# Attention probabilities turned by VectorE and a way through memory

## The reference

```
x      = rmsnorm(layernorm(x)) * w
h_q    = (x @ w_q.T).reshape(b, 128, 32, 128)      # queries
h_k    = (ctx @ w_k.T).reshape(b, 128, 32, 128)    # keys
h_v    = (ctx @ w_v.T).reshape(b, 128, 32, 128)    # values
score  = einsum('bqhd,bkhd->bhqk', h_q, h_k) + position_bias
prob   = softmax(where(mask, score, -inf), axis=-1)
attn   = einsum('bhqk,bkhd->bqhd', prob, h_v)
out    = attn @ w_out.T
```

## Time and profile before

| | us |
|---|---|
| median of 3 runs (970.29 to 971.5) | 970.51 |
| the profiled execution | 970.3 |
| its span, first to last instruction | 968.5 |
| TensorE busy | 959.6 |
| VectorE / ScalarE / GpSimd busy | 565.8 / 433.1 / 495.8 |
| one loop pass (group 3: 335.49 to 435.17) | 99.68 |

### The profile page before, as it was taken

How to read it: one execution, slowest core, us unless ns; L and a number is a source line. 1 busy time by engine, 2 the same in 40 slices (tenths; PEclk the granted TensorE clock), 3 DMA queues, 4 the chain that set the end, 5 groups by cost and what they waited for, 6 DMA issues and landing times.

```text
span 968.5 us, 15533 instructions
## 1 busy us (share of the span) xinstructions
PE 959.6 (99%) x5042; PEld 814.8 (84%) x5042; DVE 565.8 (58%) x972; ACT 433.1 (45%) x1128; POOL 495.8 (51%) x463
## 2 busy tenths in 40 slices
PE   9999899999999999999999999999999999999998
PEld 8888788888888888888888888888888888888885
DVE  5878844375437543754376436653566866756654
ACT  5774524352534343534444334433443337646630
POOL 3756653355336543745374636463546325697630
PEclk9999999999999999999999999999999999999999
DMA  7133565456555555665556555665557544200002
GB/s 280 45 131 152 205 237 222 178 218 235 205 218 206 217 217 206 238 217 217 195 219 247 217 195 195 249 238 195 195 210 281 188 158 175 88 23 1 1 1 87
DMA packets 50100, 174.28 MB, mean 180 GB/s; under 512 B 6800, under 2 KB 7056, under 8 KB 49040
## 3 DMA queue, kind: packets, MB, share of 16 engines
q1 hardware_dynamic: 49056, 172.50, 48.0%
q10 hardware_dynamic: 1008, 1.32, 0.4%
HBM read 162.26 MB, written 11.53 MB: 179 GB/s over the span
## 4 chain that ended last, share of the span: by engine, by line
PE 94%; DVE 4%; ACT 1%; DMA 1%; issue 1%; SPq 0%; DVEq 0%
PE bank L1870 27%; PE bank L1886 18%; PE bank L1939 17%; PE bank L2046 10%; PE bank L1903 6%; PE bank L1923 6%; PE bank L1846 4%; PE bank L1914 3%; PE bank L2070 2%; DVE work_raw L1426 1%; PE bank L2199 1%; PE bank L2136 1%; PE bank L2156 1%; DMA craw<-in_ctx 1%; DVE acc L1363 0%
## 5 line engine op out<-in xcount | busy, mean ns | idle before, releaser
L561 POOL TENSOR_TENSOR wvo<-stage,wvo 128x512 fp32r<-128x512 f32 x64 | 82.7, 1316 | 195.7 <-ACT wvo L862 195.7
L1939 PE MATMUL bank<-wvo,ao 128*128 128x512 f32 x768 | 180.2, 392 | 1.2 <-DVE acc L1363 1.2
L1886 PE MATMUL bank<-wvo,ct 128*128 128x512 f32 x768 | 177.8, 390 | 0.0
L1939 PEld LDWEIGHTS bank<-wvo,ao 128*128 128x128 f32 x768 | 142.9, 188 | 30.8 <-issue 1.6
L1886 PEld LDWEIGHTS bank<-wvo,ct 128*128 128x128 f32 x768 | 143.5, 188 | 29.4
L1870 PE MATMUL bank<-ring,wkq 128*128 128x512 f32 x648 | 159.0, 393 | 0.0
L1870 PEld LDWEIGHTS bank<-ring,wkq 128*128 128x128 f32 x648 | 120.2, 188 | 24.3
L1363 DVE SCALAR_TENSOR_TENSOR acc<-bank,gated_rows,acc 128x512 f32<-128x512 f32 x128 | 95.5, 748 | 48.4 <-PE bank L1939 47.7
L904 ACT ACTIVATE bank<-prob,nmax 128x128 f32<-128x128 f32 x256 | 91.4, 357 | 36.9 <-DVE nmax L1339 36.9
L1354 DVE TENSOR_TENSOR ao<-bank,ao 128x512 fp32r<-128x512 f32 x64 | 44.0, 691 | 109.3 <-ACT ao L910 109.0
L1385 DVE TENSOR_TENSOR qt<-bank,qt 128x512 f32<-128x512 f32 x98 | 66.4, 690 | 54.8 <-PE bank L1870 52.5
(11 more groups left out here) (185 smaller groups left out, 1574.1 us busy)
## 6 DMA issues: line engine op xcount, KB each, us to landing
ring<-combined SPq DMA_DIRECT2D x216, 512.0 KB, 6.2
stage<-in_w SPq DMA_DIRECT2D x63, 512.0 KB, 3.5
combined<-work SPq DMA_DIRECT2D x16, 512.0 KB, 3.4
xraw<-in_x SPq DMA_DIRECT2D x2, 1024.0 KB, 11.4
bias<-in_bias SPq DMA_DIRECT2D x8, 256.0 KB, 3.5
cs<-in_ctx SPq DMA_DIRECT2D x1, 2048.0 KB, 7.9
out<-acc SPq DMA_DIRECT2D x8, 256.0 KB, 2.0
craw<-in_ctx ACTq DMA_DIRECT2D x4, 256.0 KB, 6.1
```

Source lines behind the costliest of these rows:

```text
L561: pool.tensor_tensor(wvo[:, 1, h, :], stage[:, vo_stage(g, m, c)[0], :], wvo[:, 0, h, :].bitcast(fp32), ALU.subtract).then_inc(s_vo_lo, 1)
L1886: mm = pe.matmul(bank[un_of[m][u] % RING][:, :], ct[:, i, c, b * P:(b + 1) * P], wvo[:, j, c, :], start=(c == 0 and i + j == 0), stop=(c = ...
L1939: mm = pe.matmul(bank[to][:, :], ao[:, h, p, b * P:(b + 1) * P], wvo[:, j, 2 * pair + h, :], start=(h == 0 and p + j == 0), stop=(h == 1 a ...
```

## The change

Nothing is turned on TensorE any more, and `pt_out` is gone. Scores stay in their PSUM bank: bias and mask are added in place, the exponentials too. `softmax_out` writes the probabilities to `turned_blocks` in the order block column j, b, k, and then VectorE transposes them in squares of 32x32. To make a full transpose of these, the squares have to change places between groups of 32 partitions. That is done by a DMA to memory (`passing`, 512 KB a head, two buffers) and four DMAs back into `keyed`, each into 32 partitions. `attend` waits for these and reads `keyed`, with the 128 queries of a block as four runs of 32. `turned_blocks` and `keyed` exist once: a head's multiplication waits until the head before is in memory, and a head's way back waits for the attend of the head before.

```diff
-    prob = place("prob", [P, 2, B, P], fp32)
+    turned_blocks = place("turned_blocks", [P, 4, B, 32], fp32)
+    keyed = place("keyed", [P, 4, B, 32], fp32)
...
+    passing = nc.dram_tensor("passing", (2, 4, 32, 4, B * 32), fp32, kind="Internal").ap()
...
+                def passed(g, h):
+                    sp.wait_ge(s_turned, g * 2 * GH + 2 * h + 2)
+                    sp.dma_start(passing[h % 2, :, :, :, :].rearrange("i k j c -> (i k) j c"),
+                                 turned_blocks[:, :, :, :].rearrange("p j b q -> p j (b q)")).then_inc(s_passed, 16)
+
+                def back(g, m, h):
+                    sp.wait_ge(s_passed, 16 * (g * GH + h) + 16)
+                    if (m, h) != ("first", 0):
+                        sp.wait_ge(s_pv, g * 2 * GH + 2 * h)
+                    for j in range(4):
+                        sp.dma_start(keyed[32 * j:32 * j + 32, :, :, :].rearrange("k i b q -> k i (b q)"),
+                                     passing[h % 2, :, :, j, :].rearrange("i k c -> k i c")).then_inc(s_keyed, 16)
...
-                def pt_out(g, h):
-                    for s in range(2):
-                        act.wait_ge(s_pt, g * 2 * GH + 2 * h + s + 1)
-                        act.activation(prob[:, h % 2, 4 * s:4 * s + 4, :], bank[6 + s][:, :].rearrange("p (b k) -> p b k", b=4),
-                                       ACT.Copy).then_inc(s_pte, 1)
...
-                def softmax_out(g, h, s):
+                def softmax_out(g, m, h, s):
...
                     dve.reciprocal(rinv[:, bs], esum[:, bs]).then_inc(s_rinv, 1)
+                    if s == 0 and (m, h) != ("first", 0):
+                        dve.wait_ge(s_passed, 16 * (g * GH + h))
                     dve.wait_ge(s_rinv, n + 1)
-                    dve.tensor_tensor(prob[:, h % 2, bs, :], bank[4 + s][:, :].rearrange("p (b k) -> p b k", b=4),
-                                      rinv[:, bs].unsqueeze(2).to_broadcast([P, 4, P]), ALU.mult).then_inc(s_p, 1)
+                    dve.tensor_tensor(turned_blocks[:, :, bs, :].rearrange("p j b k -> p b j k"),
+                                      bank[4 + s][:, :].rearrange("p (b j k) -> p b j k", b=4, j=4),
+                                      rinv[:, bs].unsqueeze(2).unsqueeze(3).to_broadcast([P, 4, 4, 32]), ALU.mult).then_inc(s_p, 1)
+                    dve.wait_ge(s_p, n + 1)
+                    dve.transpose(turned_blocks[:, :, bs, :], turned_blocks[:, :, bs, :]).then_inc(s_turned, 1)
...
                 def attend(g, h):
                     if h == 0:
                         pe.wait_ge(s_val_out, 8 * g + 8)
+                    pe.wait_ge(s_keyed, 64 * (g * GH + h) + 64)
                     for s in range(2):
-                        pe.wait_ge(s_pte, g * 2 * GH + 2 * h + s + 1)
+                        pe.wait_ge(s_aolo, g * 2 * GH + 2 * h + s + 1)
                         for b in range(4 * s, 4 * s + 4):
                             mm = pe.matmul(bank[6 + s][:, (b - 4 * s) * P:(b - 4 * s + 1) * P],
-                                           vals[:, b, h * P:(h + 1) * P], prob[:, h % 2, b, :], start=True, stop=True)
+                                           vals[:, b, h * P:(h + 1) * P], keyed[:, :, b, :], start=True, stop=True)
```

The hand-written orders change with it. The second half of head 3 is multiplied right behind the first half, and `ao_lo(g, 2)` follows later, on VectorE; on TensorE the attends move: in the loop `attend(g, 0)` ahead of product P1, `attend(g, 2)` behind P1 and P6 of product 3, and in the last group `attend(g, 3)` behind `keys(2)`, right ahead of the projections:

```diff
                     if last:
                         keys(0)
-                        transposes(g, 3)
+                        attend(g, 2)
                         keys(1)
+                        keys(2)
                         attend(g, 3)
-                        keys(2)
                         for i in range(B, 2 * B):
```

More of the change, by code:

```diff
@@ L439, in _ @@
                 load(0, "o0", 1)
+                passed(0, 0)
+                back(0, "first", 0)
                 put(0, 0, 0)
@@ L442, in _ @@
                 put(0, 2, 2)
+                passed(0, 1)
+                back(0, "first", 1)
                 put(0, 3, 3)
@@ L449, in _ @@
                 put(1, 1, 3)
+                passed(0, 2)
+                back(0, "first", 2)
                 sp.wait_ge(s_vo_lo, 8)
@@ L454, in _ @@
                 put(1, 2, 2)
+                passed(0, 3)
+                back(0, "first", 3)
                 put(1, 3, 3)
@@ L471, in _, with body @@
                 load(1, "k2", 1)
-                def body(g, last):
+                def body(g, m):
+                    last = m == "last"
                     if last:
@@ L489, in body @@
                     other_pieces(prods(g, 1), 1)
+                    passed(g, 1)
+                    back(g, m, 0)
                     if last:
@@ L495, in body @@
                         load(g + 1, "k0", 0)
+                    back(g, m, 1)
                     last_piece(prods(g, 2), 1)
@@ L518, in _ @@
                 with sp.Fori(1, LAST) as g:
-                    body(g, False)
-                body(LAST, True)
+                    body(g, "loop")
+                body(LAST, "last")
                 sp.wait_ge(s_prod, last_prod)
@@ L527, in _ @@
                 sp.dma_start(fnw[:, :], a["fnw"].partition_broadcast(P)).then_inc(s_fnw, 16)
+                passed(LAST, 2)
+                back(LAST, "last", 2)
+                passed(LAST, 3)
+                back(LAST, "last", 3)
                 sp.wait_ge(s_vo_lo, vo_done(LAST, "last", "o3"))
@@ L1080, in body @@
                     vo_hi(g, "loop", "o3")
[L1081 to L1085 removed]
+                    exps(g, 3, range(2))
                     if not last:
                         first_out(g, m, 3)
[L1088 to L1089 removed]
                         vo_hi(g, "loop", "w0")
                         vo_hi(g, "loop", "w1")
[L1092 removed]
+                    ao_hi(g, 2)
+                    if last:
                         for c in range(KC):
                             split_hi("ffn", c)
[L1095 removed]
                     ao_hi(g, 3)
@@ L1905, in scores @@
                         mm.then_inc(s_s, 1)
-                def transposes(g, h):
-                    n = g * 2 * GH + 2 * h
-                    for s in range(2):
-                        pe.wait_ge(s_p, n + s + 1)
-                        pe.wait_ge(s_aolo, n + s + 1)
-                        for b in range(4 * s, 4 * s + 4):
-                            mm = pe.transpose(bank[6 + s][:, (b - 4 * s) * P:(b - 4 * s + 1) * P], prob[:, h % 2, b, :], ident[:, :])
-                        mm.then_inc(s_pt, 1)
                 def attend(g, h):
@@ L1963, in _ @@
                     value(0, "first", b)
-                transposes(0, 0)
                 scores(0, "first", 1)
@@ L1967, in _ @@
                     plain(u)
+                attend(0, 0)
                 plain("q2a")
-                attend(0, 0)
                 plain("q2b")
-                transposes(0, 1)
                 plain("q3a")
@@ L1981, in _ @@
                 project(0, "first", 7)
+                plain("k4a")
                 attend(0, 2)
-                plain("k4a")
                 plain("k4b")
-                transposes(0, 3)
                 plain("k5a")
@@ L2032, in body @@
                         return
-                    for p in ORDER[:5]:
+                    product(g, m, 3, "P1")
+                    product(g, m, 3, "P6")
+                    attend(g, 2)
+                    for p in ORDER[2:6]:
                         product(g, m, 3, p)
-                    transposes(g, 3)
-                    product(g, m, 3, "P4")
                     attend(g, 3)
```

95 lines of the change are left out of this document (40 added, 55 removed).

## The result

The changed kernel takes 1010.0 us (median of 4 runs, 1008.04 to 1012.26), the kernel before 970.78 us: 1.0404 times as long (95% interval 1.0381 to 1.0427). The forecast was 973.8 us, in a range of 956 to 993: wrong, and by 36 us. The profiled execution has a span of 1008.2 us against 968.5.

A forecast was written before the change was run, and what follows sets the result against it. TensorE, busy 99% of the span, was taken as the bound. From 970.3 us: first group +3.5 and +2.3 for the clock, six passes -1.0, last group -1.5, then 0.2 added: 973.8 us, range 956 to 993.

The forecast's parts named there:

- VectorE's part: Head 3 in a loop pass: multiplications and block transposes at 0.69 us, done 8.60 us after scores(3) starts (S).
- The write's time to landing: Head 3's 512 KB write in the loop, queued behind two fetches: lands after 4.8 us, bounds 2.6 and 5.5.
- The wait priced at its length: TensorE waits 3.4 us at attend(3) in six loop passes; 2.3 us for a slow clock only once, first group.
- Heads 0 and 1: Head 0 is in memory long before it is read; head 1 has 8.2 us between attends and needs 4.35.
- The two fetches: Two 512 KB fetches ahead of head 3's write in SyncE's queue land after 3.7 and 4.6 us; the write waits.
- The way back of head 3: Four DMAs of 128 KB from memory into keyed: 4.25 us in all, bounds 3.4 and 5.5.
- The first group: attend(3) starts at 124.3 instead of 120.74, +3.5 us, and 2.3 us more for TensorE's slow clock after idling.
- The last group: No fetches ahead of the write: a wait of 1.3 us, projections 0.8 us later, -1.5 us in sum.
- the long way: Rival: slow transposes and a 5.5 us way back make 994 us, 1010 with slow clock after each wait; chance 0.25.
- The short way: Rival: write not held by fetches (2.6 us), way back 3.6, loop wait 0.6 us; 955.7 us; chance 0.27.
- slower attends: Rival: attend matmuls reading four runs of 32 columns slow down, 10% giving 5.5 us, 979 us; chance 0.05.
- no change in effect: Rival: waits swallow exactly what is removed, 968.6 to 972.4 us; chance 0.15.

The follow-up runs named there:

- weights_behind: Changed kernel with the 768 KB of weights and bias issued behind head 3's way back, both fetches still ahead of the write; 1007.5 us.
- kept_busy: Changed kernel with 20 unused matmuls ahead of attend(3) (30 in the first group, none in the last); 996.1 us.
- no_memory: Changed kernel without the way through memory: attends read the tile VectorE turned, output not the reference's; 951.4 us.
- fetch_then_way: Changed kernel with SyncE's order: the fetch P4 reads, head 3's write and way back, then weights, bias and second fetch; 985.1 us.
- fetch_first: Changed kernel with SyncE issuing the fetch P4 reads, then head 3's write and way back, then the second fetch; 996.6 us.

## Why the prediction was wrong

- **VectorE's part: right.** Done at S+8.6, transposes of 0.71 us, exponentials of 350 ns.
- **The write's time to landing: wrong, the step that failed first.** "It can't land before the second fetch does (S+12.4), plus its own 1.2 us" holds in form; the second fetch lands at S+14.5 (430.8 + 6.7 = 437.5, S = 422.96), not at S+12.4. I took its landing from the earlier trace rows, where no write stood behind it and little ran ahead. With the write behind it, it takes 1.1 us longer (weights_behind, 5.7 us in the mean of six passes), with the weights ahead and head 2's way back still running 1.5 (6.1 in the mean; in this pass 6.7, which is 2.1 longer). My bounds of 2.6 and 5.5 both came from rows without this mixture. The write lands after 6.7 us in the mean, not 4.8, and the wait at attend(3) is 31.7 us in six passes, not 20.4: 11 us. Why fetches and a write together take so long stays open.
- **The wait priced at its length: wrong, the larger half.** I added 2.3 us for the clock in the first group "once", and gave the loop's 3.4 us none. 1.6 to 3.0 us were lost behind each of the loop's six waits, 15 us in all, and 1.7 in the first group, where 2.3 had been forecast; kept_busy gives back 14 of them. The row that led me was the start of the trace alone. The Trainium skill, TensorE: Matmul & The Clock Gate, Part 1, says that idling returns the engine to its low level. The trace agrees with it: 0.50 behind every wait of 4.7 us and more, 1.00 behind the last group's 1.3. I had confined it to one wait.
- **attend(0): missed.** Its move ahead of P1 takes the product that covered ScalarE's copy of the last value; 1.05 to 1.08 us in five passes, 1.83 in the first of them, where the wait is for head 0's way: 7 us. The order showed that move, and I had asked only whether head 1's way had time.
- **Heads 0 and 1: half wrong, at little cost.** I had written that all writes but head 3's land after 2.6 to 3.5 us. Head 1's stands behind six fetches and takes 8.2 to 9.5 in the loop, and head 0's way back beside it 10.0 to 11.5 from its first issue. In pass 3 it landed at 399.39, 0.35 us ahead of attend(0).
- **The two fetches: half understood.** I looked only at the six fetches for the next group, which the projections cover. One of the two ahead of the write is read in the same product, and that is why moving the write ahead of it did not help.
- **The way back of head 3: right.** 4.37 us pass from the first issue to the last landing, forecast 4.25. Head 2's, forecast alike, takes 5.0 to 5.8 in the loop, so the 0.95 us it had to spare became a wait of 0.26 in this pass.
- **The first group: right.** attend(3) at 124.63 for 124.3, and the next group starts 5.6 us later for 5.8. (Two roundings of the working, 12.4 + 1.2 as 13.5 and 4.5 - 2.12 as 2.3, are 0.1 us short and change nothing.)
- **The last group: its terms right.** The wait is 1.33 for 1.3, and the projections start 0.81 later for 0.8. What was missed is attend(0) again (0.85); another 0.8 us is spread over the group, 0.34 of it at a product that reads `ring`.

Of the rivals, the long way ended at 1010 us, the time measured. It had the clock right; but its price for the way, 20 us, came from slow transposes and a slow way back of head 3, and these were neither, while the late write (11 us) and attend(0) (7 us) were not in it. That its total agrees is luck. Its chance of 0.25 against 0.43 was the misjudgement: the forecast sat 0.16 us a pass from the point where waits outweigh savings. The short way is refuted by the landing, slower attends by 275 to 278 ns each in no_memory, no change in effect by the time itself.

## What to carry to other kernels

When a transfer is put onto the path, take its time from rows in which the same traffic stands ahead and behind, reads and writes mixed; a lone landing was a lower bound here, and the transfers ahead got later too. Here a wait of 4.7 us or more on TensorE cost 1.6 to 3.0 us beyond its length, so price the granted clock behind it, or keep the engine busy. Before moving a transfer in a queue, look up which of the transfers it passes is read soonest; and where one of several alike units has no cover, leave that one on the old path.

## What the hardware showed that I had not expected

- Head 3's write of 512 KB lands 2.6 us after its issue with no fetch right ahead of it (once 3.3), after 3.4 to 3.7 with one 512 KB fetch issued 1.2 us ahead, after 5.9 to 6.1 with two (once 7.7). Three writes in a row need 5.2 us in all, two fetches and a write 7.1 to 7.4.
- The length of a wait alone does not tell whether the clock falls. In fetch_then_way, at attend(3), waits of 2.57 us (first window) and 2.81 left it at 1.00, while those of 2.10 to 2.38 at the same place in the other four passes brought it to 0.50. In fetch_first 1.88 us at attend(0), behind the value matmuls, did so too (second window, 0.70 in the mean):

```profile
432.70:434.40 1.70, 1.70 (x15) 1.00 0.92 340
```
```profile
188.50:191.20 2.70, 2.70 (x17) 0.70 0.02 6
```

- VectorE turns the 32 x 32 blocks of 128 x 512 fp32 in 0.71 us; adding as many numbers takes it 0.69.
